# Zero fill on ScalarE, and twelve first results added before the last stage of a graph and mixture-of-experts kernel

## The chip, the cores and the metric

The kernel runs on one core of a Trainium2 chip. The metric is the device time of one execution in microseconds (us). It was timed three times; a separate execution was profiled. One core has TensorE (PE, matmul), VectorE (DVE), ScalarE (ACT), GpSimd (POOL) and SyncE (SP), which each run their own instruction stream and meet at semaphores, and 16 DMA engines.

## The reference

```python
x = x + gnn(layernorm(x), weight, bias, edge_index, edge_type)      # 3125 nodes x 256, 53125 edges, 8 relations
x = x + ffn(layernorm(x)[None], gate_w, gate_b, w1, w2, w3)[0]

def gnn(node_repr, weight, bias, edge_index, edge_types):
    h_all = jnp.einsum('ni,roi->rno', node_repr, weight)
    msgs = h_all[edge_types, src]
    return jax.ops.segment_sum(msgs, dst, num_segments=3125) + bias

def ffn(x, gate_w, gate_b, w1, w2, w3):                             # 16 experts, hidden 512
    probs = softmax(x @ gate_w + gate_b); top_probs, top_idx = top_k(probs, 2)
    top_probs = top_probs / sum(top_probs)
    hidden = silu(x @ w1[e]) * (x @ w2[e])
    return sum over the two experts e of a node of top_probs[e] * (hidden @ w3[e])
```

Every node thus gets its row after the graph layer, plus two weighted rows that its two experts computed.

## The kernel before

The 3125 nodes are handled as 25 node tiles (`TILES`) of 125 rows (`TP`). The work has four stages.

- **Start, about 0 to 72 us of the profile.** SP loads x into `acc` (five batches of five tiles) and the edge lists. VectorE turns a first list of edge sources (`early_src`) into floats (L959), TensorE turns them to partitions (L1544), VectorE writes them as indices `early_idx` (L965), and that releases GpSimd's first 37 indirect gathers of rows of x (L617: 25 into `held`, in the tile `part`, and 12 into `odd_held`). VectorE and ScalarE normalize the rows, in a high and a low half of 16 bits each, into `got`; SP stores them as a table `x_tab` and then loads the relation weights (L471). Part of this is the moments of the first ten gathered tiles (`held_moments(0)`, L1031), which VectorE computes before the edge keys and the last two batches of x. GpSimd also sets constants, and it clears `ffn` (L601, the zeros that are later stored over the table `y_tab`) and `logit` (L602).
- **Graph layer, to about 560 us.** One turn for each node tile: GpSimd gathers up to 17 chunks of 125 neighbour rows (L611), TensorE multiplies them with one-hot matrices (L1593), VectorE adds the windows into `store`, TensorE applies the relation weights (L1605).
- **Experts, to about 890 us.** Nodes are sorted by expert into slot tiles of 128 rows, in this input 58 of them (`final_j` is the last). `expert_tile` stands in the code of TensorE, ScalarE and VectorE, one call for each slot tile. In VectorE's, `low_hid` (L1442) works on the tile before, then `hid` is formed (L1454), `low_xs` (L1432) prepares the next tile, and `copy_y` (L1438) takes the result of the tile before out of PSUM bank 4. In ScalarE's, `high_hid` (L874), `store_y` (the DMA of a result tile to `y_tab`, L890), the Silu (L885), and `high_xs` (L868). TensorE's up product is L1759, its down product L1741, its turning of `hid` L1767. The experts use PSUM banks 0 to 4.
- **Sum, to the end.** `y_tab` holds a row for each (node, expert) pair. GpSimd gathers each node tile's lower row into `y1` (L694) and its higher row into `y2` (L707). For each node tile t ScalarE copies `acc` to PSUM (`keep_sum`, L920), VectorE adds the first result there (`add_first`, L1510) and then the second one into `acc` (`add_second`, L1519). SP stores 112 rows of the tile (L583) and ScalarE 13 rows (L929). `SUM_BANK` names the six PSUM banks for this, with one tile in each, so that add_first is ahead of add_second by four tiles. No bank beyond the experts' own is used for it before the last result was copied out: ScalarE issues the last `store_y` before the first `keep_sum`.

All engines work through their streams in the order in which the code is written; a wait holds everything that stands behind it on that engine.

## Time and profile before

| | before |
|---|---|
| median of 3 runs | 914.04 us (911.89 to 915.19) |
| the profiled execution's own time | 916.64 us |
| its span, first to last instruction | 914.8 us |
| busy: PE / POOL / DVE / ACT | 731.6 / 655.4 / 518.1 / 302.4 us |
| mean granted TensorE clock | 0.944 |

The span is 1.84 us shorter than the time of its own execution, and that execution was 2.60 us above the median of the three timed runs. Busy times are sums over stages in which different engines set the pace, so they do not say by themselves what one stage is worth.

### The profile page before, as it was taken

What the parts mean: (1) busy time and instruction counts of PE and PEld (TensorE: products, weight loads), DVE (VectorE), ACT (ScalarE), POOL (GpSimd) and SP (SyncE); (2) the same over time, 40 slices, a digit from 0 to 9 for tenths busy, and PEclk for the clock granted to TensorE, in tenths of its full rate; (3) what the DMA queues carried; (4) which work ended last, traced back from release to release, by engine and by line L of the source; (5) the groups of instructions that cost most, each with busy time, mean ns of one, the idle gap of its engine ahead of it and who ended that gap; (6) DMA issues with size and microseconds to landing.
All of it is one profiled execution on the core that took longest, in us unless ns stands there. A gap on an engine that the chain in (4) does not pass through costs nothing.

```text
span 914.8 us, 19945 instructions
## 1 busy us (share of the span) xinstructions
PE 731.6 (80%) x4626; PEld 623.0 (68%) x4627; DVE 518.1 (57%) x1444; ACT 302.4 (33%) x469; POOL 655.4 (72%) x609
## 2 busy tenths in 40 slices
PE   0136697888788898888879888689999999999980
PEld 0125586777677676777758676467888888788870
DVE  6887566545556446555446767874444444344438
ACT  5524234332333323343233523122333333233323
POOL 7777777777777777777777740359787886987772
PEclk9998799999999999999979998999999999999995
DMA  9875656433333333333364324176656655663546
GB/s 203 250 229 179 189 184 199 142 106 105 106 107 108 107 105 105 106 108 105 108 187 132 104 65 167 30 266 200 212 189 218 229 184 187 200 215 93 163 133 187
DMA packets 92526, 142.09 MB, mean 155 GB/s; under 512 B 13752, under 2 KB 67069, under 8 KB 92476
## 3 DMA queue, kind: packets, MB, share of 16 engines
q0 software_dynamic: 25440, 69.50, 26.1%
q1 hardware_dynamic: 50114, 56.92, 19.6%
q10 hardware_dynamic: 16922, 15.15, 5.2%
q14 instruction: 38, 0.31, 0.1%
q8 instruction: 12, 0.20, 0.1%
HBM read 108.59 MB, written 32.93 MB: 155 GB/s over the span
## 4 chain that ended last, share of the span: by engine, by line
PE 45%; POOL 22%; issue 14%; DMA 10%; DVE 7%; ACT 1%; DVEq 0%; POOLq 0%; SPq 0%; ACTq 0%
POOL got L611 20%; PE ps L1759 16%; PE ps L1741 9%; PE ps L1593 8%; PE ps L1605 6%; DMA got<-x_tab,gidx 6%; PE ps L1767 3%; DMA store<-in_L_gnn_weight 2%; PE ps L1725 1%; PE ps L1694 1%; DVE ps L1510 1%; POOL part L617 1%; DMA y_tab<-ffn 1%; DMA part<-in_x,early_idx 1%; POOL part L645 1%
## 5 line engine op out<-in xcount | busy, mean ns | idle before, releaser
L611 POOL DMA_INDIRECT got<-x_tab,gidx x383 | 366.4, 957 | 118.3 <-issue 108.9
L1593 PE MATMUL ps<-hot,got 125*128 125x256 f16 x1680 | 219.3, 290 | 79.7 <-DMA got<-x_tab,gidx 75.7
L1593 PEld LDWEIGHTS ps<-hot,got 125*128 125x128 f16 x1680 | 170.1, 104 | 122.9 <-issue 38.4
L1156 DVE TENSOR_TENSOR store<-store,ps 128x512 f32 x150 | 102.6, 684 | 179.2 <-PE ps L1593 146.2
L1759 PE MATMUL ps<-part,operands 128*128 x696 | 179.3, 407 | 4.9 <-DVE operands L1432 3.1
L1605 PE MATMUL ps<-part,store 128*128 128x256 f32 x800 | 181.9, 386 | 0.5 <-DVE acc L1167 0.5
L1605 PEld LDWEIGHTS ps<-part,store 128*128 128x128 f32 x800 | 152.5, 193 | 20.7 <-issue 0.6
L1759 PEld LDWEIGHTS ps<-part,operands 128*128 128x128 f32 x696 | 128.3, 191 | 32.5 <-issue 5.7
L1138 DVE TENSOR_SCALAR hot<-key_row,pass,drel 125x256 f16<-125x256 f16 x425 | 126.1, 362 | 7.5 <-ACT store L778 4.9
L1741 PE MATMUL ps<-part,operands 128*128 x696 | 97.9, 289 | 3.8 <-DVE operands L1442 3.6
L645 POOL TENSOR_TENSOR part<-store,part 128x2048 fp32r<-128x2048 f32 (+1 forms) x28 | 98.0, 3500 | 2.3
L787 ACT ACTIVATE dev<-mv,eps 125x1 f32<-125x1 f32 x25 | 7.4, 295 | 257.8 <-DVE mv L1174 257.8
L1741 PEld LDWEIGHTS ps<-part,operands 128*128 128x128 f32 x696 | 87.0, 189 | 4.5 <-issue 4.5
L1454 DVE TENSOR_TENSOR ffn<-ffn,ps 128x512 f32<-128x512 f32 x58 | 39.9, 687 | 83.1 <-PE ps L1759 79.4
L656 POOL DMA_INDIRECT x_sb<-x_tab,oct_idx x56 | 54.8, 979 | 21.8 <-issue 16.7
L804 ACT COPY store<-store 128x2480 f32<-128x2480 f32 x24 | 54.2, 2259 | 31.8 <-DVE store L1156 31.8
L874 ACT CAST operands<-ps 128x512 fp32r<-128x512 f32 x58 | 34.0, 587 | 91.7 <-PE ps L1767 91.7
L1442 DVE TENSOR_TENSOR operands<-ps,operands 128x512 fp32r<-128x512 f32 x58 | 40.0, 690 | 26.8 <-ACT operands L874 26.7
L885 ACT ACTIVATE ffn<-ps 128x512 f32<-128x512 f32 x58 | 34.7, 598 | 59.0 <-PE ps L1759 49.8
L1438 DVE COPY ffn<-ps 128x256 f32<-128x256 f32 x58 | 24.6, 425 | 51.1 <-PE ps L1741 31.1
L643 POOL TENSOR_SCALAR part<-store 128x2048 fp32r<-128x2048 f32 (+1 forms) x28 | 41.6, 1485 | 15.4 <-PE ps L1759 14.4
L782 ACT COPY store<-zero 128x2000 f32<-128x2000 f32 x25 | 46.9, 1875 | 0.0
(254 smaller groups left out, 685.8 us busy)
## 6 DMA issues: line engine op xcount, KB each, us to landing
store<-in_L_ffn_w SPq DMA_DIRECT2D x48, 512.0 KB, 4.8
part<-x_tab SPq DMA_DIRECT2D x625, 1.0 KB
y_tab<-ffn SPq DMA_DIRECT2D x9, 896.0 KB, 6.3
y_tab<-ffn ACTq DMA_DIRECT2D x58, 128.0 KB
xs_tab<-x_sb SPq DMA_DIRECT2D x14, 512.0 KB, 3.3
ffn<-xs_tab ACTq DMA_DIRECT2D x55, 128.0 KB
got<-x_tab,gidx POOLq DMA_INDIRECT x383, 2.8
acc<-in_x SPq DMA_DIRECT2D x5, 560.0 KB
```

The costliest lines, as they stand in the source:

```text
L611: nc.gpsimd.indirect_dma_start(got[:, c, :], None, x_tab, bass.IndirectOffsetOnAxis(ap=gidx[:, col:col + 1], axis=0)).then_inc(gathered[g] ...
L643: nc.gpsimd.tensor_scalar(high, whole, 1.0, 0.0, ALU.mult, ALU.add).then_inc(split_high, 1)
L645: nc.gpsimd.tensor_tensor(part[:, 2 * k + 1, at:at + cols], whole, high.bitcast(F32), ALU.subtract).then_inc(done, 1)
L656: nc.gpsimd.indirect_dma_start(xg[:, u, :], None, x2_tab, bass.IndirectOffsetOnAxis(ap=oct_idx[:, u:u + 1], axis=0)).then_inc(oct_got[u // ...
L782: nc.scalar.copy(buffer(i, SPAN - TP, SPAN), zero[:, 0:1].unsqueeze(1).to_broadcast([P, KT * RELS, TP])).then_inc(tail_clear, 1)
L804: nc.scalar.copy(buffer(i + 1, 0, SPAN - TP), buffer(i, TP, SPAN)).then_inc(moved_on, 1)
L1138: made = v.tensor_scalar(hot[0:CE, g % HOT, c - GROUPS[g][0], :], key_row[0:CE, :], pass0[0:CE, 0:1], drel[0:CE, bass.ds(turn * TC + c, 1) ...
L1156: v.tensor_tensor(window, window, ps[:, WIN_BANK[g], :].rearrange("p (q n) -> p q n", n=WIN), ALU.add).then_inc(win_added, 1)
L1593: last = mm(ps[:, WIN_BANK[g], k * KEYS:(k + 1) * KEYS], rows, hot[0:CE, g % HOT, c - c0, :], start=(c == c0 and a == 0), stop=(c == c1 - ...
L1605: last = mm(ps[:, bank, 0:DIM], sums[:, at, k, r, 0:P], wT[:, k, r * DIM:(r + 1) * DIM], start=(r == 0 and k == 0), stop=(r == RELS - 1 an ...
L1741: last = mm(ps[:, Y_BANK, 0:DIM], hidT[:, a, k, :], part3[:, bass.ds(at + b, 1), k, :].rearrange("p a n -> p (a n)"), start=(k == 0 and a ...
L1759: last = mm(ps[:, UP_BANK + w, :], xsT[:, a, k, :], part12[:, bass.ds(at + b, 1), w, k, :].rearrange("p a n -> p (a n)"), start=(k == 0 an ...
```

## The change

First, GpSimd's two memsets of `ffn` and `logit` are removed and ScalarE writes the same zeros, by copying a broadcast zero. Second, the sums are held two to a PSUM bank (`SUMS` = 12 places, `sum_at`), and ScalarE copies `acc` to PSUM two tiles at a time (`keep_sums`). Twelve tiles get their `add_first` earlier: three after `low_hid` in each of the last two expert tiles, five after the last `low_hid`, and one after the last `copy_y`. In what is left add_first is ahead by eight tiles. VectorE's and ScalarE's last pair of expert tiles stand behind their loops for it. The diff:

```diff
@@ -417,6 +417,8 @@
         WIN_BANK, MSG_BANK, T_BANK, GATE_BANK = (0, 1, 2, 5, 6, 7), 3, 4, 4
         UP_BANK, XS_BANK, HID_BANK, Y_BANK = 0, 2, 3, 4
         SUM_BANK = (5, 6, 7, 0, 1, 2)
+        SUMS = 2 * len(SUM_BANK)
+        SOON_SUMS = 3
 
         CHOICE_STEPS = 6
         SWEEP_STEPS = 2 * CHOICE_STEPS + 7
@@ -430,6 +432,10 @@
         def buffer(i, n0, n1):
 
             return sums[:, bass.ds(i % 2, 1), :, :, n0:n1].rearrange("p a k r n -> p (a k r) n")
+
+        def sum_at(t):
+            n = t % SUMS
+            return ps[0:TP, SUM_BANK[n // 2], n % 2 * DIM:(n % 2 + 1) * DIM]
 
         def low_hot(k, t):
 
@@ -598,8 +604,6 @@
             nc.gpsimd.iota(tile_i[:, :, :], pattern=[[1, TILES], [0, NG]], base=0, channel_multiplier=0).then_inc(iota_ready, 1)
             nc.gpsimd.iota(token_i[:, 0:2 * TILES], pattern=[[0, 2], [1, TILES]], base=-(TILES // 2), channel_multiplier=0).then_inc(iota_ready, 1)
             nc.gpsimd.iota(token_i[:, 2 * TILES:], pattern=[[0, 1]], base=0, channel_multiplier=1).then_inc(iota_ready, 1)
-            nc.gpsimd.memset(ffn[:, :], 0.0).then_inc(zeros_set, 1)
-            nc.gpsimd.memset(logit[:, :, :], 0.0).then_inc(acc_init, 1)
 
             def gather_turn(n, turn):
                 for g, (c0, c1) in enumerate(GROUPS):
@@ -718,6 +722,8 @@
             for n in range(2):
                 act.sem_inc(xs_in[n], (n + 1) * 16)
             act.wait_ge(zero_set, 1)
+            nc.scalar.copy(ffn[:, :], zero[:, 0:1].to_broadcast([P, ZT * DIM])).then_inc(zeros_set, 1)
+            nc.scalar.copy(logit[:, :, :].rearrange("p t e -> p (t e)"), zero[0:TP, 0:1].to_broadcast([TP, TILES * EXPERTS])).then_inc(acc_init, 1)
 
             def spread_x(n):
 
@@ -885,6 +891,14 @@
                 nc.scalar.activation(gate, ps[:, UP_BANK, :], ACT.Silu).then_inc(gate_ready, 1)
                 act.wait_ge(up2_done, j + 1)
                 high_xs(j + 1, 1 - u, load=load and not first)
+            def keep_sums(q):
+
+                t0, t1 = 2 * q, min(2 * q + 2, TILES)
+                if t0 >= SUMS:
+                    act.wait_ge(out_ready, t0 - SUMS + 2)
+                bank = ps[0:TP, SUM_BANK[q % len(SUM_BANK)], 0:(t1 - t0) * DIM].rearrange("p (t d) -> p t d", d=DIM)
+                nc.scalar.copy(bank, acc[:, t0:t1, :]).then_inc(first_sum, 1)
+
             def store_y(j):
                 act.wait_ge(y_ready, j + 2)
                 act.dma_start(y_tab[bass.ds(j * P, P), :], y_sb).then_inc(y_stored, 16)
@@ -901,31 +915,30 @@
             with act.Fori(1, early + (LAST_PAIRS - 1)) as i:
                 for u in range(2):
                     expert_tile(i, u)
-            for u in range(2):
-                expert_tile(early + (LAST_PAIRS - 1), u, load=False)
+            keep_sums(0)
+            keep_sums(1)
+            expert_tile(early + (LAST_PAIRS - 1), 0, load=False)
+            keep_sums(2)
+            expert_tile(early + (LAST_PAIRS - 1), 1, load=False)
             act.wait_ge(y_done, final_j + 1)
             high_hid(final_j)
             store_y(final_j - 1)
+            act.wait_ge(hid_ready, final_j + 1)
+            act.sem_inc(tiles_begun, 1)
+            act.wait_ge(xsT_ready, final_j + 2)
+            act.sem_inc(tiles_begun, 1)
+            for q in range(3, 6):
+                keep_sums(q)
             store_y(final_j)
             act.wait_ge(xs_in[0], pairs * 16)
             act.wait_ge(xs_in[1], pairs * 16)
             act.sem_inc(tiles_begun, 1)
 
-            banks = len(SUM_BANK)
-
-            def keep_sum(t):
-
-                if t >= banks:
-                    act.wait_ge(out_ready, t - banks + 1)
-                nc.scalar.copy(ps[0:TP, SUM_BANK[t % banks], 0:DIM], acc[:, t, :]).then_inc(first_sum, 1)
-
             p0, p1 = SPREAD[1]
-            for t in range(banks):
-                keep_sum(t)
             for t in range(TILES):
                 act.wait_ge(out_ready, t + 1)
-                if t + banks < TILES:
-                    keep_sum(t + banks)
+                if t % 2 and t - 1 + SUMS < TILES:
+                    keep_sums((t - 1 + SUMS) // 2)
                 act.dma_start(out[t * TP + p0:t * TP + p1, :], acc[p0:p1, t, :]).then_inc(out_stored, 16)
             act.wait_ge(y_stored, (pairs * 2 + 1) * 16)
             act.sem_inc(tiles_begun, 1)
@@ -1442,10 +1455,12 @@
                 v.tensor_tensor(hidT[:, 1, :, :], ps[:, HID_BANK, :].rearrange("p (k n) -> p k n", k=HT),
                                 hidT[:, 0, :, :].bitcast(F32), ALU.subtract).then_inc(hidT_ready, 1)
 
-            def expert_tile(i, u, first=False, tables=None):
+            def expert_tile(i, u, first=False, firsts=(), tables=None):
                 j = i * 2 + u
                 if not first:
                     low_hid(j - 1)
+                    for t in firsts:
+                        add_first(t)
                     if tables:
                         tables()
                 dve.wait_ge(gate_ready, j + 1)
@@ -1459,7 +1474,7 @@
                     copy_y(j - 1)
 
             final_j = dve.value_load(final[0:1, 0:1], min_val=0, max_val=SLOT_TILES - 1)
-            pairs = dve.value_load(pairs_i[0:1, 0:1], min_val=EXPERTS // 2, max_val=SLOT_TILES // 2)
+            early = dve.value_load(early_i[0:1, 0:1], min_val=EXPERTS // 2 - LAST_PAIRS, max_val=SLOT_TILES // 2 - LAST_PAIRS)
             low_xs(0)
             order_tables()
             positions()
@@ -1505,27 +1520,30 @@
 
             def add_first(t):
                 dve.wait_ge(y_got[t], 16)
-                dve.wait_ge(first_sum, t + 1)
-                at = ps[0:TP, SUM_BANK[t % len(SUM_BANK)], 0:DIM]
-                v.scalar_tensor_tensor(out=at, in0=y1[0:TP, t, :], scalar=wts2[:, 0, t:t + 1],
-                                       in1=at, op0=ALU.mult, op1=ALU.add).then_inc(part_done, 1)
-
-            with dve.Fori(3, pairs) as i:
+                dve.wait_ge(first_sum, t // 2 + 1)
+                v.scalar_tensor_tensor(out=sum_at(t), in0=y1[0:TP, t, :], scalar=wts2[:, 0, t:t + 1],
+                                       in1=sum_at(t), op0=ALU.mult, op1=ALU.add).then_inc(part_done, 1)
+
+            with dve.Fori(3, early + (LAST_PAIRS - 1)) as i:
                 for u in range(2):
                     expert_tile(i, u)
+            for u in range(2):
+                expert_tile(early + (LAST_PAIRS - 1), u, firsts=range(u * SOON_SUMS, (u + 1) * SOON_SUMS))
+
             def add_second(t):
                 dve.wait_ge(part_done, t + 1)
                 dve.wait_ge(y_got[t], 2 * 16)
                 v.scalar_tensor_tensor(out=acc[:, t, :], in0=y2[0:TP, t % YR, :], scalar=wts2[:, 1, t:t + 1],
-                                       in1=ps[0:TP, SUM_BANK[t % len(SUM_BANK)], 0:DIM], op0=ALU.mult, op1=ALU.add).then_inc(out_ready, 1)
+                                       in1=sum_at(t), op0=ALU.mult, op1=ALU.add).then_inc(out_ready, 1)
 
             low_hid(final_j)
+            for t in range(2 * SOON_SUMS, SUMS - 1):
+                add_first(t)
             copy_y(final_j)
-            ahead = len(SUM_BANK) - 2
-            for t in range(ahead):
-                add_first(t)
+            add_first(SUMS - 1)
+            ahead = SUMS - 4
             for t in range(TILES):
-                if t + ahead < TILES:
+                if SUMS <= t + ahead < TILES:
                     add_first(t + ahead)
                 add_second(t)
 
```

The order of instructions shows three places; line numbers behind the change are up to 18 higher. First GpSimd's stream at its start, where the gathers of `early_idx` come; before:

```order
L597 IOTA hot 128x256
L598 IOTA tile_i 1x150
L599 IOTA token_i 128x50
L600 IOTA token_i 128x1
L601 MEMSET ffn 128x1792
L602 MEMSET logit 125x400
L617 DMA part<-in_x,early_idx 128x256 x25
```

And GpSimd's stream in the changed kernel:

```order
L603 IOTA hot 128x256
L604 IOTA tile_i 1x150
L605 IOTA token_i 128x50
L606 IOTA token_i 128x1
L621 DMA part<-in_x,early_idx 128x256 x25
L621 DMA odd_held<-in_x,early_idx 128x256 x12
```

The two memsets are gone. ScalarE's stream begins, in the changed kernel, with them and a table load of their own, where it began with the load and the square root:

```order
L725 ACT_TABLE_LOAD
L725 COPY ffn<-zero 128x1792 [waits zero_set]
L726 COPY logit<-zero 125x400
L732 ACT_TABLE_LOAD
L732 ACTIVATE dev<-mv,eps 125x5 [waits stats_done]
```

Two copies and one table load were added ahead of the first real work. Second, VectorE's stream around the last `low_hid` (L1442) and the last `copy_y` (L1438); before:

```order
L1442 TENSOR_TENSOR operands<-ps,operands 128x512
L1436 REGISTER_ALU
L1437 REGISTER_ALU
L1438 COPY ffn<-ps 128x256
L1510 SCALAR_TENSOR_TENSOR ps<-x_sb,wts,ps 125x256 x5
L1519 SCALAR_TENSOR_TENSOR acc<-store,wts,ps 125x256
L1510 SCALAR_TENSOR_TENSOR ps<-x_sb,wts,ps 125x256
```

And in the changed kernel, from the last tile's `low_hid` (L1455) on:

```order
L1455 TENSOR_TENSOR operands<-ps,operands 128x512
L1524 SCALAR_TENSOR_TENSOR ps<-x_sb,wts,ps 125x256 x5
L1449 REGISTER_ALU
L1450 REGISTER_ALU
L1451 COPY ffn<-ps 128x256
L1524 SCALAR_TENSOR_TENSOR ps<-x_sb,wts,ps 125x256
L1536 SCALAR_TENSOR_TENSOR acc<-store,wts,ps 125x256 x4
L1524 SCALAR_TENSOR_TENSOR ps<-x_sb,wts,ps 125x256
L1536 SCALAR_TENSOR_TENSOR acc<-store,wts,ps 125x256
```

Five first adds moved ahead of the last copy, and one stands behind it; two groups of three stand further up, between `low_hid` and `hid` of the last two tiles. Third, ScalarE's stream of the changed kernel from the end of its loop of expert tiles, with what each instruction waits for:

```order
L915 COMPARE_AND_BRANCH
L900 COPY ps<-acc 125x512 x2
L885 ISA
L880 CAST operands<-ps 128x512 [waits hid_turned,y_done]
L904 ISA [waits y_ready]
L904 DMA y_tab<-ffn 128x256
L889 REGISTER_ALU
L891 ACTIVATE ffn<-ps 128x512 [waits hid_ready,up1_done]
L873 REGISTER_ALU [waits up2_done]
L874 CAST operands<-ps 128x256 [waits xs_turned]
L900 COPY ps<-acc 125x512
L880 CAST operands<-ps 128x512 [waits hid_turned,y_done]
```

Two double copies now stand ahead of `high_hid` of the last tile but one, and one ahead of that of the last tile; three more come before the last `store_y`.

## Rows read from the trace of the kernel before

**Rows 1.** The page, part 4: the chain that ended last, by engine.

```profile
PE 45%; POOL 22%; issue 14%; DMA 10%; DVE 7%; ACT 1%; DVEq 0%; POOLq 0%; SPq 0%; ACTq 0%
```

**Rows 2.** Timeline, 2 to 8 us: start, duration, instruction, [idle before, its releaser].

```profile
2.74 2.20 DVE L959 CAST store<-store 37x125 f32<-37x125 int32 x1 [0.70 <-DMA store<-in_src]
...
2.92 1.58 POOL L601 MEMSET ffn<- 128x1792 f32 x1
...
4.45 0.42 POOL L602 MEMSET logit<- 125x400 f32 x1
...
6.01 1.16 POOL L617 DMA_INDIRECT part<-in_x,early_idx  x1 [1.14 <-DVE early_idx L965]
```

**Rows 3.** Timeline of DVE, 0 to 75 us.

```profile
25.69 3.37 DVE L1031 BATCH_NORM_STATS2 stat<-part 125x6 f32<-125x256 f32 x10 [3.55 <-DMA part<-in_x,early_idx]
...
29.64 0.45 DVE L1018 CAST store<-store 85x625 f32<-85x625 int32 x1
```

**Rows 4.** DMA issues in 6.0 to 6.2 and 17.6 to 17.8 us; last number: us to landing.

```profile
part<-in_x,early_idx POOLq DMA_INDIRECT x1, 8.8
...
part<-in_x,early_idx POOLq DMA_INDIRECT x1, 8.0
```

**Rows 5.** The chain that ended last, 0 to 110 us: start, duration, what.

```profile
46.00 16.96 DMA store<-in_L_gnn_weight
```

**Rows 6.** Waits of POOL over the whole span: us in total, times, longest.

```profile
POOL got L611 <- issue: 108.9, 357, 0.3
...
POOL got L611 <- PE ps L1593: 9.4, 26, 1.8
```

**Rows 7.** Timeline of ACT, 0 to 75 us.

```profile
9.22 1.28 ACT L726 ACT_TABLE_LOAD   x1 [9.22 <-DVE mv L983]
...
71.60 3.92 ACT L778 COPY store<-zero 128x4480 f32<-128x4480 f32 x1 [1.65 <-issue]
```

**Rows 8.** Timeline of DVE, 855 us to the end.

```profile
879.79 0.69 DVE L1454 TENSOR_TENSOR ffn<-ffn,ps 128x512 f32<-128x512 f32 x1 [1.49 <-PE ps L1759]
...
890.26 0.42 DVE L1438 COPY ffn<-ps 128x256 f32<-128x256 f32 x1 [2.18 <-PE ps L1741]
891.91 2.05 DVE L1510 SCALAR_TENSOR_TENSOR ps<-x_sb,wts,ps 125x256 f32<-125x256 f32 x5 [1.22 <-ACT ps L920]
893.87 0.47 DVE L1519 SCALAR_TENSOR_TENSOR acc<-store,wts,ps 125x256 f32<-125x256 f32 x1
...
909.71 2.04 DVE L1519 SCALAR_TENSOR_TENSOR acc<-store,wts,ps 125x256 f32<-125x256 f32 x5
```

**Rows 9.** Timeline of ACT, 855 us to the end (ACTq: its DMA issues).

```profile
875.39 0.35 ACTq L864 DMA_DIRECT2D ffn<-xs_tab  x1
876.99 0.59 ACT L874 CAST operands<-ps 128x512 fp32r<-128x512 f32 x1 [1.50 <-PE ps L1767]
...
886.98 4.22 ACTq L890 DMA_DIRECT2D y_tab<-ffn  x2
891.41 1.90 ACT L920 COPY ps<-acc 125x256 f32<-125x256 f32 x6 [4.05 <-DVE ffn L1438]
...
894.45 0.60 ACTq L929 DMA_DIRECT2D out<-acc  x1
```

**Rows 10.** Timeline of PE, 855 us to the end.

```profile
888.40 1.73 PE L1741 MATMUL ps<-part,operands 128*128 x12 [1.72 <-DVE operands L1442]
```

**Rows 11.** Instructions on `y_tab`, 830 to 915 us: duration, first and last start; landing.

```profile
L694 POOL DMA_INDIRECT x_sb<-y_tab,pos x25: 942/946/999, 835.6 to 865.7; - x25
L707 POOL DMA_INDIRECT store<-y_tab,pos x25: 942/946/949, 866.9 to 898.5; - x25
...
DMA to landing us min/median/max: 2.7/2.9/4.1
```

**Rows 12.** SP's out stores, 910.2 us to the end; windows, with DMA share and GB/s last.

```profile
910.21 2.49 SPq L583 DMA_DIRECT2D out<-acc  x5
...
900.00:902.00 2.00, 0.00 (x0) 0.00 (x0) 2.00 (x6) 1.04 (x3) 0.00 (x0) 0.50 0.92 283
```

## The prediction

> **What bounds the kernel now.** I read the page's chain first, then the timeline of every engine at the two places that the change touches. The chain [rows 1] shows TensorE and GpSimd as the two long parts: GpSimd's gathers through the graph layer, TensorE through the experts. VectorE has 7%, most of it after the last expert tile. The change touches neither long part; it touches what comes before and behind them. So the two questions are whether an earlier start is handed on through some 840 us, and what bounds the last 25 us.
>
> *Start.* GpSimd's train of gathers begins at 6.01 us and waited 1.14 us for VectorE's `early_idx` [rows 2]. The reader should look at what held VectorE: its cast L959 covers only 37x125 numbers, yet takes 2.20 us and ends at 4.94. A cast of 85x625, five times as many in each row, takes 0.45 us [rows 3]. Beside the slow one stand GpSimd's two memsets, from 2.92 to 4.87 us [rows 2]; the cast ends 0.07 us after the second. I read it as one engine being held by the other until the memsets end. The Trainium skill, "SBUF — State Buffer", section "Who interferes with whom", says that certain VectorE copies and casts and any GpSimd instruction take one shared port pair exclusively, and whoever comes second is fully blocked; the trace agrees in that 2.20 against 0.45 us.
>
> From there the chain runs on. VectorE is idle 3.55 us until the tenth gather has landed, at 25.69 [rows 3]. That gather was issued at 17.65 and took 8.0 us, the first one 8.8 [rows 4]; so the time to land hardly depends on when a gather is issued, though the queues are full then. Behind it come edge keys, the last batches of x, and at 46.00 the relation weights, 16.96 us on the path [rows 5]. In the graph layer GpSimd's gathers wait 357 times 0.3 us for nothing the profile shows, and for TensorE only 9.4 us in all [rows 6]: the train is nearly back to back, TensorE follows it, and nothing there is tied to a fixed time.
>
> *End.* After the last `copy_y` at 890.26 VectorE has 50 adds to do and no idle gap worth the name: first ones at 891.91, last ones from 909.71 for 2.04 us, so to 911.75 [rows 8]. One add takes 0.47 us but starts (2.04 - 0.47) / 4 = 0.39 us after the one before. Stores follow; the span ends at 914.8, 3.05 us after the last add. The last y2 gather starts at 898.5, and the longest landing is 4.1 us [rows 11]: it is there by about 902.6, nine us before it is used. VectorE is the bound.
>
> **The change part by part.**
>
> *Memsets off GpSimd.* They end at 4.87 while GpSimd cannot gather before 6.01, so their own time is hidden; the worth is in the cast. With GpSimd's iotas over by 2.92 to 3.0 us, the cast (issued at 2.74) should end at about 3.05 in place of 4.94. The rest, transpose, copy, semaphores, took 6.01 - 4.94 = 1.07 us and stays. First gather at about 4.1: 1.9 us earlier. From below: nothing, if the cast is slow for a reason of its own, or if the queues, full of loads of x, land the tenth gather no sooner. From above: the idle time that waits for the gather, 3.55 us. I take 1.9, since the latencies of 8.8 and 8.0 us [rows 4] are near enough to constant, and 1.9 is less than 3.55. After that it is carried on, since each later step on the chain is released by the one before.
>
> *Zeros on ScalarE.* 4480 columns took 3.92 us there [rows 7]; 1792 and 400 columns at that rate are 1.57 and 0.35 us, with the new table load of 1.28 us some 3.3 us in all, from about 2 us on (or the load even earlier). ScalarE's first work is at 9.22 us, having waited 9.22 us [rows 7]. Cost nothing; the cover is about 3.9 us.
>
> *Copies in the last two tiles (ScalarE).* A copy of 256 columns takes about (1.90 - 0.38) / 5 = 0.30 us more than the one before [rows 9], a double one, with 256 more columns at 3.92 / 4480 us each, about 0.53. Two of them begin when the DMA issue of 875.39 is over, at 875.74, and end near 876.9. `high_hid` starts at 876.99, after 1.50 us of idle time [rows 9]. If the exit from the loop adds some tenths, `high_hid` is late by that; behind it queue a store and the Silu, and VectorE's `low_hid` waits for it. TensorE would feel it only when its slack is gone, and it is busy with the up products then. Cost 0, bound 0.5 us.
>
> *Three adds in each of the two tiles (VectorE).* 3 x 0.39 = 1.2 us in an idle gap of 1.49 us ahead of `hid` [rows 8]. Hidden, by 0.3 us. The `hid` instruction (0.69 us) would be late next if the gap does not hold, and TensorE's turning behind it. Bound 0.5 us for each tile.
>
> *Five adds after the last `low_hid`.* TensorE's last down product starts at 888.40 and takes 1.73 us [rows 10]; VectorE is idle 2.18 us before `copy_y` [rows 8]. The adds need 5 x 0.39 = 1.95 us from about 888.2, once ScalarE's three double copies (from 887.4, after the store issued at 886.98) give them their places: to 890.2. `copy_y` is not late, or by 0.1 us. The last `store_y` now stands behind three copies that end at about 889.1; it is issued at 890.9 anyway.
>
> *The rest.* Before, VectorE went from `copy_y` (890.26) to the first add at 891.91, since ScalarE had to store and to copy first, 1.22 us of it idle [rows 8]. Now the twelfth add comes at about 890.60. Gain 1.31 us. Adds left: 50 - 11 = 39, so 11 x 0.39 = 4.3 us less. A new wait: after four second adds the thirteenth first add needs a double copy that ScalarE may start only when two second adds are done (891.9) and its first store of a row is issued (0.60 us [rows 9]): ready near 892.9, wanted at 892.56. Cost 0.35 us. Later copies have four adds of lead. Last add ends at 911.75 - 1.31 - 4.3 + 0.35 = 906.5 or a little less; y2 is there since 902.6.
>
> *Stores.* With eight tiles ahead, the last nine second adds come 0.39 us apart, where before it was five. SP issued its last five stores from 910.21 to 912.70, one in 2.49 / 5 = 0.50 us [rows 12]: slower than 0.39. Before it fell back by 4 x 0.11 = 0.4 us; now 8 x 0.11 = 0.9. Cost 0.5 us. The most that the queues moved at this stage is 283 GB/s at a share of 0.92 [rows 12]; nine tiles of 125 KB in 9 x 0.39 us would be 328. Queues that can't follow cost 9 x 128 / 283 = 4.1 us for 3.5, another 0.6 us; it overlaps the first, and I take 0.5 for both, bound 1.5.
>
> **The sum.** Start -1.9; first add earlier -1.3; eleven adds -4.3; new wait +0.35; stores +0.5: -6.7 us, with the small bounds above at nothing. The profiled execution goes from 916.64 to about 909.9 (span 914.8 to 908.1). The median of the runs shown stood 2.60 us below that execution, so 914.04 becomes 907.4. Of the three runs, two differ by 3.3 us; less than 0.3% (2.7 us) cannot be told from no change here.
>
> **The rivals.**
>
> *The start gives nothing back* (0.15). For it: while x is loaded the queues are full, and a gather needs 8 us; if it lands when the loads issued ahead have drained, an earlier issue is only a longer wait. Against: the first gather and the tenth have nearly the same latency. Only the end is left: 914.04 - 4.8 = 909.2 us. The same time results if the cast stays slow.
>
> *The end becomes a matter of stores* (0.13). SP's 0.50 us and the queues' 283 GB/s, with y2 gathers still beside them, set the pace instead of the adds: bound 1.5 us in place of 0.5, perhaps another 0.5 from the four early second adds. 908.4 to 908.9 us.
>
> *The insertions reach TensorE* (0.07). `high_hid` and `hid` late in both tiles, 0.5 us each time, `copy_y` late too: +1 to +1.5 us, so 908.4 to 909 us.
>
> *The adds do no good where they stand* (0.02): if add 6 to 11 wait for ScalarE until `copy_y`, that is late and their time comes back: +2 us and more, with a lost start about 911.5, within 0.3%.
>
> *Slower* (0.02). VectorE's stream now waits for y1 of tiles 0 to 5 inside the last expert tiles; `hid`, `low_xs` and TensorE stand behind that wait. Were the sixth y1 gather to land after about 879.4 us, each us of it would go on the path; slower by 0.3% needs a landing 6.7 + 2.7 us later, at about 888.8. The gathers start at 835.6 and 25 take until 865.7 [rows 11], so the sixth starts near 841.9 and with 4.1 us has landed at 846. Cover 33 us: only a much later y table would bring it about. It would give 917 us and up.
>
> **How the numbers follow.** My forecast, both gains whole, has 0.61: 907.4, alone from 906.2 (less lost at the stores, a start gain of 2.2) to 908.6. The range is to hold 8 in 10 and takes in the lost start and the store case: 905.3 to 910.2, which leaves out the adds case and the slower one, and runs beyond the mean of three runs by about 1 us on the low side. Faster by over 0.3% (below 911.3): the first four cases, 0.95; within 0.3%: 0.03; slower: 0.02.
>
> **What the changed profile would show.** Right: the cast of 37x125 under 0.5 us, the first gather near 4.1, VectorE's moments (L1031 before) near 23.8, the weights issued near 44.1, the whole graph layer and the experts some 1.9 us earlier; in the last two tiles no idle time of TensorE before its turning of `hid`; then 0.35 us idle at the thirteenth first add, and a last add some 5.2 us earlier relative to the last `copy_y` of before. Wrong: a cast that still takes 2 us; a tenth gather that lands at 25.7 with 10 us latency; TensorE gaps near 880; SP's stores still being issued 2 us after the last add. A run of the granted clock that falls elsewhere in the graph layer could shift the total by a us or two with none of these steps wrong.

## The result, and the profile after

The changed kernel takes 910.42 us (median of 12 runs), the kernel before 915.18 us (12 runs, 911.9 to 920.4). One of the twelve runs of the changed kernel took 1263 us (without it the median is 909.84, and the range 905.0 to 913.6), and in two of the four groups of experiments below every kernel, the one before too, took some 1200 us for a reason that no run tried, so times are compared inside a group only. The ratio is 0.9947, with a 95% interval of 0.9928 to 0.9966: 4.85 us faster, and anything from 3.1 to 6.6. The forecast was 907.4 with a range from 905.3 to 910.2, a gain of 6.7 us. The direction was right. The median of the twelve lies 0.2 us above the range, that of the eleven 0.4 us inside it, so the time alone hardly says whether the sum was wrong. A part of the distance is the base: the three runs shown before had a median of 914.04, the twelve of the comparison 915.18.

The profiled execution of the changed kernel took 911.70 us with a span of 909.3, against 916.64 and 914.8. So there are 5.5 us to be found in the two traces. I read the start first. These rows are from the engines' timelines after the change, 0 to 80 us (SPq: SyncE's DMA issues), in order of time.

```profile
1.30 1.28 ACT L725 ACT_TABLE_LOAD   x1 [1.30 <-PEq L1830]
2.75 0.22 DVE L972 CAST store<-store 37x125 f32<-37x125 int32 x1 [0.70 <-DMA store<-in_src]
4.03 1.16 POOL L621 DMA_INDIRECT part<-in_x,early_idx  x1 [1.03 <-DVE early_idx L978]
5.89 19.27 SPq L466 DMA_DIRECT2D acc<-in_x  x4
24.62 3.37 DVE L1044 BATCH_NORM_STATS2 stat<-part 125x6 f32<-125x256 f32 x10 [3.84 <-DMA part<-in_x,early_idx]
37.29 1.09 ACT L745 ACTIVATE got<-acc,shift_n,rstd 125x256 f16<-125x256 f32 x2 [1.20 <-DMA x_tab<-got]
44.38 1.65 ACT L753 COPY store<-ps 1x425 f32<-1x425 f32 x2
45.93 0.84 SPq L477 DMA_DIRECT2D store<-in_L_gnn_weight  x1
62.09 6.12 PE L1575 MATMUL ps<-ident,store 128*128 128x128 f32 x32 [10.21 <-DMA store<-in_L_gnn_weight]
66.70 2.23 ACT L761 COPY part<-ps 128x512 f32<-128x512 f32 x4
71.26 9.00 PE L1611 MATMUL ps<-hot,got 125*128 125x256 f16 x54 [3.05 <-DVE hot L1151]
74.81 0.94 POOL L615 DMA_INDIRECT got<-x_tab,gidx  x1 [3.12 <-PE ps L1611]
```

The cast takes 0.22 us where it took 2.20 [rows 2]. It still starts at 2.75, beside GpSimd's last iotas, and no memset is there to hold it. The first gather starts at 4.03 in place of 6.01. Both are as forecast. The Trainium skill, "SBUF — State Buffer", section "Who interferes with whom", says that a VectorE copy or cast that uses both port pairs and a GpSimd instruction shut each other out of the shared pair, and that the one that issues first gets it. The traces agree with the first half, by 2.20 against 0.22 us. They don't show the second: before the change the cast starts at 2.74 and the first memset at 2.92, and yet the cast is the one that is held.

Then the lead of 2 us wears off, in two places. The first is the landing of the gathers. The tenth is issued at 15.50, 2.15 us earlier than before, but it takes 9.1 us to land in place of 8.0 [rows 4]. In every profile near 910 us that has the early gathers and where the tenth one's landing can be read it took 8.5 to 9.1 us, in e2, which hasn't them, 7.7:

```profile
part<-in_x,early_idx POOLq DMA_INDIRECT x1, 9.1
```

So the moments behind it are at 24.62, only 1.07 us earlier than [rows 3] has them. The second place is SyncE's stores of `x_tab`. SyncE is done with issuing its last four loads of x at 25.16 in place of 24.34. In the eight profiles near 910 us that have the early gathers this is at 24.6 to 25.4 us, in the two without them at 23.8 and 24.3; I put it down to the gathers' packets on the same DMA engines, which were busy without a gap from 6 to 24 us already before the change (DMA share 1.02 to 1.12). So the stores of `x_tab` are later, and ScalarE has a wait that it didn't have before, 1.20 us, until 37.29. At its copy of the edge lines, which releases VectorE's planning of the graph layer, it stands at 44.38; before that was

```profile
44.47 1.64 ACT L747 COPY store<-ps 1x425 f32<-1x425 f32 x2
```

The lead at that place is 0.09 us, and SyncE issues the relation weights at 45.93, before at 46.00 [rows 5]: 0.07 us. The train of GpSimd's gathers, which doesn't wait for that copy, goes on 2 us early until about 70 us, then stands 3.12 us before the first gather of the second turn, because TensorE's first window (71.26, before 72.27) has not freed a buffer. Before the change it stood there too:

```profile
75.82 0.95 POOL L611 DMA_INDIRECT got<-x_tab,gidx  x1 [1.83 <-PE ps L1593]
```

The first window starts 2.3 us after the last of ScalarE's eight copies of the turned weights, in this profile (68.93 to 71.26) and in all ten near 910 us. In both profiles here those copies wait for the weights, which TensorE could use 16.2 us after their issue, and before the change 17.0 us after it. So the 1.0 us by which the window leads comes mostly from a load that happened to be faster and not from the gathers. From there GpSimd leads by 1.0 us, by 1.1 at the end of the graph layer, and by 0.5 when the last `hid` of the experts is made (884.19, before 884.68).

The end, from VectorE's timeline:

```profile
882.62 1.26 DVE L1524 SCALAR_TENSOR_TENSOR ps<-x_sb,wts,ps 125x256 f32<-125x256 f32 x3
884.19 0.69 DVE L1469 TENSOR_TENSOR ffn<-ffn,ps 128x512 f32<-128x512 f32 x1 [0.31 <-issue]
...
887.79 2.06 DVE L1524 SCALAR_TENSOR_TENSOR ps<-x_sb,wts,ps 125x256 f32<-125x256 f32 x5 [0.20 <-ACT ps L900]
889.76 0.42 DVE L1451 COPY ffn<-ps 128x256 f32<-128x256 f32 x1
890.10 0.48 DVE L1524 SCALAR_TENSOR_TENSOR ps<-x_sb,wts,ps 125x256 f32<-125x256 f32 x1
890.49 1.65 DVE L1536 SCALAR_TENSOR_TENSOR acc<-store,wts,ps 125x256 f32<-125x256 f32 x4
892.42 0.49 DVE L1524 SCALAR_TENSOR_TENSOR ps<-x_sb,wts,ps 125x256 f32<-125x256 f32 x1 [0.28 <-ACT ps L900]
```

The three adds lie in the gap before `hid`, with 0.31 us left of the 1.49 of [rows 8]. Five more lie before the last `copy_y`, which comes 5.57 us after the last `hid`, as before (890.26 - 884.68 = 5.58). The thirteenth add waits 0.28 us. The last add ends at 905.83, 16.07 us after `copy_y` started; before it was 911.75 - 890.26 = 21.49. The span ends 3.45 us behind the last add, where it was 3.03. From the last `hid` to the end of the span it is 25.1 us, and was 30.1: the end gives 5.0 us. With 0.5 of lead left at that `hid`, this is the 5.5 between the traces.

### The profile page after: what moved, and what is told of

The parts are those of the page before. It is cut to its first block, busy times and chain, and to the rows that moved or that the text cites. A ratio compares the mean times of both kernels' runs of the same rounds, so it can differ in the third digit from the quotient of the medians.

```text
span 909.3 us, 19921 instructions
## 1 busy us (share of the span) xinstructions
PE 733.3 (81%) x4626; PEld 622.9 (69%) x4627; DVE 517.1 (57%) x1444; ACT 303.4 (33%) x460; POOL 652.9 (72%) x607
## 4 chain that ended last, share of the span: by engine, by line
PE 47%; POOL 17%; issue 13%; DMA 9%; DVE 8%; SPq 3%; ACT 1%; DVEq 1%; POOLq 0%; ACTq 0%
POOL got L615 16%; PE ps L1777 16%; PE ps L1611 9%; PE ps L1759 8%; PE ps L1623 8%; DMA got<-x_tab,gidx 6%; PE ps L1785 3%; SPq L466 2%; DMA y_tab<-ffn 2%; PE ps L1743 1%; PE ps L1712 1%; DMA x_tab<-got 1%; DVE acc L1536 1%; DVE hot L1151 1%; ACT got L745 1%
## 5 line engine op out<-in xcount | busy, mean ns | idle before, releaser
L891 ACT ACTIVATE ffn<-ps 128x512 f32<-128x512 f32 x58 | 34.7, 598 | 62.8 <-PE ps L1777 46.2
L1455 DVE TENSOR_TENSOR operands<-ps,operands 128x512 fp32r<-128x512 f32 x58 | 40.1, 691 | 26.8 <-ACT operands L880 26.7
L1451 DVE COPY ffn<-ps 128x256 f32<-128x256 f32 x58 | 24.6, 425 | 52.0 <-PE ps L1759 29.2
```

## The experiments

There were sixteen runs of eight kernels, in four groups (e1 to e4, e5 to e8, e9 to e12, e13 to e16); those of one group share a chip and the runs of the kernel before. Each profile gives two marks to compare by: ScalarE's line copy near 44 us (how early the graph layer can be planned) and the stretch from the last `hid` to the end of the span (what the end costs).

**e1: the kernel before with the zero fill alone.**

```diff
-            nc.gpsimd.memset(ffn[:, :], 0.0).then_inc(zeros_set, 1)
-            nc.gpsimd.memset(logit[:, :, :], 0.0).then_inc(acc_init, 1)
...
+            nc.scalar.copy(ffn[:, :], zero[:, 0:1].to_broadcast([P, ZT * DIM])).then_inc(zeros_set, 1)
+            nc.scalar.copy(logit[:, :, :].rearrange("p t e -> p (t e)"), zero[0:TP, 0:1].to_broadcast([TP, TILES * EXPERTS])).then_inc(acc_init, 1)
```

> The kernel before with only the zero fill moved to ScalarE. Theory A: the first gather goes at 4.03 us as in the changed kernel, but the lead of 2 us shrinks to about 1 us at the first window of the graph layer (71.3 in place of 72.3), because SP's loads of x take 0.8 us longer and the table stores behind them land late; total 0.5 to 1.1 us under the kernel before. Rival 1: the lead is carried on whole, total 1.9 us under. Rival 2: nothing is left, total within 0.3 us.

912.03 us against 913.29: ratio 0.9986 (0.9966 to 1.0007), so 1.3 us faster, between 3.1 faster and 0.6 slower. The cast takes 0.22 us, the first gather is at 4.02, the moments at 24.65, and again there is the new wait and no lead at the line copy:

```profile
37.58 1.09 ACT L739 ACTIVATE got<-acc,shift_n,rstd 125x256 f16<-125x256 f32 x2 [0.99 <-DMA x_tab<-got]
44.66 1.65 ACT L747 COPY store<-ps 1x425 f32<-1x425 f32 x2
```

The interval holds the theory (0.5 to 1.1 us), the lead carried on whole (1.9 us) and nothing at all, so the time doesn't decide between them.

**e2: the changed kernel with the memsets back on GpSimd** (the reverse of e1's edit).

> The changed kernel with the two memsets back on GpSimd. Theory A: the end's gain is whole by itself: from the last copy_y to the last add 16.1 us in place of 21.5, and 3.4 us from there to the end in place of 3.05; total 5.0 us under the kernel before. The cast of 37x125 takes 2.2 us again. Rival: the end's gain needs the start's, or is partly lost at the stores: 3.5 us or less under.

910.5 us, ratio 0.9962 (0.9942 to 0.9983): 3.5 us faster than before (1.6 to 5.3). Last `hid` to end 25.1 us, as in the changed kernel: the end's gain doesn't need the start's. The cast takes its 2.21 us again, so with e1 it is shown that the memsets beside it make it slow:

```profile
2.74 2.21 DVE L972 CAST store<-store 37x125 f32<-37x125 int32 x1 [0.69 <-DMA store<-in_src]
```

ScalarE does not wait for `x_tab<-got`, as in the kernel before, and its line copy is at 44.05, earlier than in the changed kernel. Its relation weights happen to land by 59.95, and the first window starts at 69.91; the kernel before has the same instructions up to there and needs until 72.27. So single profiles differ by 2 us at the first window, and the lead of 1.0 us seen there is no proof.

**e3: the changed kernel with three small loads later**, after the third store of `x_tab` in place of ahead of the first.

```diff
-            sp.dma_start(bias[:, :], ...).then_inc(small_in, 16)
-            sp.dma_start(gw_sb[:, :, :], ...).then_inc(small_in, 16)
-            sp.dma_start(gb_sb[:, :], ...).then_inc(small_in, 16)
...
+                if n == 2:
+                    sp.dma_start(bias[:, :], ...).then_inc(small_in, 16)
+                    sp.dma_start(gw_sb[:, :, :], ...).then_inc(small_in, 16)
+                    sp.dma_start(gb_sb[:, :], ...).then_inc(small_in, 16)
```

> The changed kernel with SP's three small loads (bias, gate weights, gate bias) issued after the third store of x_tab instead of ahead of the first. Theory A: they stood for 2.3 us ahead of the stores (25.20 to 27.48 us), so the first store lands 1 to 2 us earlier, ScalarE's wait of 1.20 us at 37.29 is gone, the lead at 44.4 us becomes about 1.1 in place of 0.1, and the first window starts near 70.3; total about 1 us under the changed kernel. Rival: the queues are full, the store lands at the same time for its bytes, and nothing changes (within 0.3 us).

907.08 us (7 runs), ratio 0.9935 (0.9907 to 0.9964). The wait of ScalarE is gone and the line copy is at 43.47. So about 1 us of the lead does die at the stores of `x_tab`, and can be had back there. Whether it is worth anything in the whole is e15's question.

**e4: no adds inside the last two tiles** (`SOON_SUMS = 0`: the six adds go behind the last `low_hid`).

> The changed kernel with no first adds inside the last two expert tiles: eleven of them after the last low_hid instead of five. Theory A: eleven need 4.3 us where 2.1 are free, so the last copy_y starts 2.3 us late and the total is 2.3 us over the changed kernel, that is 2.7 us under the kernel before; this says that the six adds inside the tiles are hidden and worth their 0.39 us each. Rival: the end is bound by stores, so that the late adds cost less than 1 us.

909.57 us, ratio 0.9961 (0.9940 to 0.9982). The eleven adds in one piece make `copy_y` late:

```profile
887.06 4.40 DVE L1524 SCALAR_TENSOR_TENSOR ps<-x_sb,wts,ps 125x256 f32<-125x256 f32 x11
891.37 0.42 DVE L1451 COPY ffn<-ps 128x256 f32<-128x256 f32 x1
```

It starts 7.62 us after the last `hid` in place of 5.57, and the end takes 27.3 us in place of 25.1. So the place inside the tiles is worth 2.1 us by the profiles. The last tiles stand 4.89 us apart at `hid` with the adds inside and without them, so they cost nothing there. The times are too near to show it: 910.5 for e2, whose end has the adds inside but whose start is the old one, and 909.57 here.

**e5 to e12: four kernels, twice.** In these two groups the kernel before took 1204.1 and 1203.4 us, and the first window of the graph layer stood at 98 to 104 us, so nothing of the start is read from them. The kernels were: the relation weights' load moved up (e5, e9; see e13), two buffers for y (e6, e10; see e14), the out stores of tiles 17 to 22 in three pairs (e7, e11), these three all with e3's edit too, and the change as it is (e8, e12).

```diff
-            for t in range(TILES):
-                sp.wait_ge(out_ready, t + 1)
-                sp.dma_start(out[t * TP + p0:t * TP + p1, :], acc[p0:p1, t, :]).then_inc(out_stored, 16)
+            for t, n in OUT_PARTS:
+                sp.wait_ge(out_ready, t + n)
+                sp.dma_start(out[t * TP:(t + n) * TP, :].rearrange("(t p) d -> p t d", p=TP)[p0:p1, :, :],
+                             acc[p0:p1, t:t + n, :]).then_inc(out_stored, 16)
```

The edit shown is that of e7 and e11 on SyncE; ScalarE's stores have the same one. What was expected, in the order e5 to e12:

> The changed kernel with the small loads after the third store of x_tab (as in e3) and, right behind them, the load of the relation weights (w_raw), which stood at the end of SyncE's list. Theory 'the start's lead dies at the weights': in four profiles the weights' first transposes stand at 60 to 63 us while the work ahead of them is done at 44 us, so the first window at 70 to 72 us is set by when the weights land. With the load some 3 us after the x loads they should be there by 50 us, TensorE's transposes should stand at 50 us or earlier, the first window should stand at 68.5 to 70 us (then VectorE's chain holds it), and the kernel should be 1 to 2 us below e3 with less spread. Rival 'the full queues only change places': the 1.3 MB or so in front of the last two x_tab stores makes these and the gathers of got that wait for them later by as much, the first window stays at 70.5 to 72, and the time is that of e3 within 1 us or above it.

> The changed kernel with the small loads later (as in e3) and two buffers for the results y of a slot tile (the second is xn2, free by then), each with its own semaphore, so that VectorE's copy of tile j waits for the store of tile j-2 in place of j-1. Theory 'the run-to-run loss in the expert phase is VectorE behind late y stores': the copies' waits on DMA y_tab<-ffn vanish from the trace, the stretch from hid of tile 4 to hid of tile 37 falls from 162.3 us (e3) to 33 x 4.89 = 161.4 us, the one at tiles 0 to 4 from 25.4 us by some 2 us, and the kernel is 2 to 4 us below e3 (903 to 905). Rival 'PE sets the pace': the waits vanish and TensorE's tiles stand at the same distance as before, within 1 us of e3. Second rival: SyncE's and GpSimd's weight loads of the next expert, which the stores wait behind, are what is late, and the stall moves to the gate or to the splits of the weights: no gain either, but a new wait is named at hid.

> The changed kernel with the small loads later (as in e3) and the out stores of tiles 17 to 22 issued as three pairs instead of six, on each of the two queues; it moves the same bytes. From the last add to the end of the span e3 takes 3.54 us. If the predicted +0.5 us at the end is issue-bound (each issue on SyncE takes about 0.5 us, and the last ones stand in line behind each other), the stretch falls to about 3.0 and the kernel by 0.5 us. If it is the transfer itself and its landing, the stretch stays at 3.4 to 3.6 and the time is that of e3.

> The changed kernel once more, on the same chip as e5 to e7, as the bar for them. Theory: 0.5% below the kernel before, 909.5 to 911.5 us if this chip is like the first one; first window at 70 to 72 us with a wait of ScalarE on x_tab<-got at 37 us of 0.9 to 1.3 us; last add to end 3.5 us, last copy of y to last add 16.1 us.

> The kernel of e5 once more. On the chip of e5 to e8 every kernel took some 1200 us: SyncE's loads of far rows took 20 to 27 us a turn there in place of 10 to 11, and the graph layer waited for them, so nothing at the start could be read. On a chip where the kernel before takes some 914 us the expectations of e5 stand: theory, weights' transposes at 50 us or earlier, first window at 68.5 to 70 us, 1 to 2 us below the kernel of e3; rival, first window at 70.5 to 72 us and no gain, or a loss, because the load stands in front of the last x_tab stores.

> The kernel of e6 once more, for the same reason. Theory: no wait of the copy of y for DMA y_tab<-ffn, the stretch from hid of tile 4 to hid of tile 37 at 161.4 us or less, hid 0 to hid 4 shorter by about 2 us, 2 to 4 us below e3's kernel. First rival: TensorE sets the pace and the time stays within 1 us. Second rival: a new wait takes the place, named at hid or at the splits of the weights.

> The kernel of e7 once more, for the same reason. There the stretch from last add to end was 3.72 us with pairs and 3.54 with single stores, 1 run each, so now I take it that pairs bring nothing: 3.4 to 3.8 us and the time of e3's kernel within its interval. If issues bound the end it would be 3.0.

> The kernel of e8 once more, as the bar for e9 to e11 on their chip: 0.3 to 0.7% below the kernel before; copy of y to last add 16.1 us, last add to end 3.5 us, ScalarE's wait for x_tab<-got at 37 us of 0.9 to 1.3 us, first window at 70 to 72 us.

The stretch from the last `hid` to `copy_y` is not steady there (5.56 to 7.76 us), but what stands behind `copy_y` is as it was. Last add to end of span: 3.72 and 3.50 us with pairs, 3.57 and 3.48 with single stores (e8, e12). With pairs SyncE's last issue starts 0.13 us after the last add, with single stores 0.96 and 0.87 us after it, and the end doesn't come earlier, so the 3.5 us are not set by SyncE's issues. The ratios tell little: e5 1.0019 (0.9986 to 1.0053) and e9 1.0002 (0.9965 to 1.0040), e6 0.9981 (0.9956 to 1.0006) and e10 0.9994 (0.9959 to 1.0029), e7 0.9973 (0.9944 to 1.0003), e11 0.9993 (0.9957 to 1.0029), e8 0.9986 (0.9954 to 1.0018), e12 0.9954 (0.9911 to 0.9997). Copy of y to last add is 16.06 or 16.07 us in all eight. e5, e6, e9 and e10 were run again at some 910 us, as e13 and e14; e7 and e11 were not.

**e13: the relation weights' load early**, right behind e3's small loads.

```diff
                 if n == 2:
...
+                    sp.dma_start(w_raw, w_rel.rearrange("r (a p) i -> p (r a) i", p=P)).then_inc(w_in, 16)
-            sp.dma_start(w_raw, w_rel.rearrange("r (a p) i -> p (r a) i", p=P)).then_inc(w_in, 16)
```

> The kernel of e5. Theory: weights' transposes at 50 us or earlier, first window at 68.5 to 70 us, 1 to 2 us below e15. Rival: the load stands in front of the last x_tab stores, the first window is at 70.5 us or later, and the time is e15's or above. In the runs at 1200 us the rival's sign was there: first window at 103 us against 98 us without the edit.

912.66 us, ratio 0.9991 (0.9975 to 1.0007), in a group where the kernel before took 914.19: 5.4 us slower than e15, the same kernel without this edit. The rival won, and more clearly than I had put it. TensorE's and GpSimd's timelines:

```profile
52.51 5.90 PE L1576 MATMUL ps<-ident,store 128*128 128x128 f32 x28 [1.78 <-DMA store<-in_L_gnn_weight]
65.27 1.11 PE L1576 MATMUL ps<-ident,store 128*128 128x128 f32 x4 [6.87 <-ACT part L762]
69.33 6.84 PE L1612 MATMUL ps<-hot,got 125*128 125x256 f16 x36 [2.95 <-DVE hot L1152]
...
58.23 0.95 POOL L616 DMA_INDIRECT got<-x_tab,gidx  x1 [5.91 <-issue]
```

The weights are there at 52.5 in place of 60.4, and the first window moves by 0.45 us only (e15: 69.78): their last transposes now wait for VectorE's moments, by way of ScalarE. But the first gather of `got`, which needs all of `x_tab`, starts at 58.23, where e15 has

```profile
52.64 1.18 POOL L616 DMA_INDIRECT got<-x_tab,gidx  x1 [0.30 <-issue]
```

The profile puts the 5.91 us down to "issue"; that it is the last stores of `x_tab` behind the 2 MB of weights is what the edit shows, since nothing else was moved. These 5.6 us stay: the first gather of the second turn is 5.3 us later than in e15 (78.63 against 73.34), the last one of the layer 5.5 us (538.97 against 533.48). In this kernel GpSimd goes through the second turn without a wait for TensorE, so what bounds the graph layer here is when the first gather of `got` starts. In the changed kernel it is not: there GpSimd waits 3.12 us at that place, and the second turn starts 3.55 us behind the first window. The two traces agree in that the later of the two sets the layer's pace from there.

**e14: two buffers for y**, each with a semaphore, on top of e3.

```diff
-        y_sb = ffn[:, 2 * HIDDEN:2 * HIDDEN + DIM]
+        y_sb = (ffn[:, 2 * HIDDEN:2 * HIDDEN + DIM], xn2[:, :])
...
-            def copy_y(j):
+            def copy_y(j, u, i):
                 dve.wait_ge(y_done, j + 2)
-                dve.wait_ge(y_stored, (j + 1) * 16)
-                v.tensor_copy(y_sb, ps[:, Y_BANK, 0:DIM]).then_inc(y_ready, 1)
+                dve.wait_ge(y_stored[u], (i + 1) * 16)
+                v.tensor_copy(y_sb[u], ps[:, Y_BANK, 0:DIM]).then_inc(y_ready, 1)
```

> The kernel of e6. Theory: no wait of the copy of y for DMA y_tab<-ffn, hid of tile 4 to hid of tile 37 at 161.4 us, hid 0 to hid 4 down by about 2 us, 2 to 4 us below e15. Rival: TensorE sets the pace (its tiles stand 4.89 us apart), the waits go and the time stays within 1 us of e15.

906.68 us (6 runs), ratio 0.9916 (0.9894 to 0.9937): the same as e15 and e16. The groups by line, VectorE, 590 to 908 us, busy and mean ns, then idle time and its releasers; e16 (the change as it is) first, e14 second:

```profile
L1469 DVE TENSOR_TENSOR ffn<-ffn,ps 128x512 f32<-128x512 f32 x58 | 39.8, 687 | 76.0 <-PE ps L1777 72.8 <-ACT ffn L891 2.6 <-issue 0.6
L1451 DVE COPY ffn<-ps 128x256 f32<-128x256 f32 x58 | 24.6, 424 | 52.0 <-PE ps L1759 27.5 <-DMA y_tab<-ffn 24.6
```

```profile
L1474 DVE TENSOR_TENSOR ffn<-ffn,ps 128x512 f32<-128x512 f32 x58 | 39.8, 687 | 82.3 <-PE ps L1782 81.7 <-issue 0.6
L1456 DVE COPY ffn<-ps 128x256 f32<-128x256 f32 x29 | 12.3, 424 | 18.1 <-PE ps L1764 18.1
L1456 DVE COPY xn<-ps 128x256 f32<-128x256 f32 x29 | 12.3, 424 | 19.2 <-PE ps L1764 19.2
```

24.6 us of waits for stores of y are gone, and came back in part as waits for TensorE. From `hid` of tile 4 to that of tile 37 it is 162.2 us in e14, 162.7 in e16 and 162.3 in e3. So the waits for stores cost nothing that can be seen, and TensorE's pace is what is left; I had taken the late stores for 2 to 4 us, and that was wrong.

**e15 and e16: e3's kernel and the change as it is, in the group of e13 and e14.**

> The kernel of e3: ScalarE's wait for x_tab<-got at 37 us gone, its line copy at 43.5 us, 0 to 3 us below e16 (e3 stood 0.12% under the change's own first ratio, with intervals of 0.3 to 0.4%).

> The changed kernel as it is: 0.3 to 0.7% below the kernel before, last copy of y to last add 16.1 us, last add to end 3.5 us, ScalarE's wait for x_tab<-got at 37 us of 0.9 to 1.3 us, first window at 70 to 72 us.

e15: 907.22 us (6 runs), ratio 0.9928 (0.9902 to 0.9954). e16: 906.89 us (6 runs), ratio 0.9921 (0.9902 to 0.9939). In ScalarE's timelines, e16 then e15, the small loads cost what they cost before:

```profile
37.18 1.09 ACT L745 ACTIVATE got<-acc,shift_n,rstd 125x256 f16<-125x256 f32 x2 [1.12 <-DMA x_tab<-got]
44.26 1.65 ACT L753 COPY store<-ps 1x425 f32<-1x425 f32 x2
```

```profile
35.91 1.09 ACT L746 ACTIVATE got<-acc,shift_n,rstd 125x256 f16<-125x256 f32 x2 [0.20 <-DMA x_tab<-got]
43.15 1.65 ACT L754 COPY store<-ps 1x425 f32<-1x425 f32 x2
```

1.1 us of lead at 43 us, and no difference between the medians that could be told from none. So no version that beats the changed kernel was found.

## Why the prediction was off, step by step

*What the cast waits for, and the first gather*: right (0.22 us, 4.03 us; 0.22 and 2.21 in e1 and e2). *Zeros on ScalarE at no cost*: right. Its two copies and the second table load end at 6.0 us, and its first work starts at 9.19, where it was 10.52 before, since that load no longer stands in front of it.

*The start's term, -1.9 us*: this is what failed, in both of its premises. "I take 1.9, since the latencies of 8.8 and 8.0 us are near enough to constant": the tenth gather was issued 2.15 us earlier and landed 1.07 us earlier, after 9.1 us in place of 8.0. "After that it is carried on, since each later step on the chain is released by the one before": the later steps are not all behind the gathers. Some are behind the loads and stores of x, which share the queues with the gathers. The weights were to be issued near 44.1; they were at 45.93, before at 46.00, and at 45.6 in e2, whose gathers are not early. In the profiles with early gathers (after, e1, e4, e16) the line copy is at 44.38, 44.66, 44.19 and 44.26, with ScalarE's new wait of 1.0 to 1.2 us in each; in the two without (before, e2) it is at 44.47 and 44.05, without that wait. Of 2.0 us nothing is left there. The bound "if the queues, full of loads of x, land the tenth gather no sooner" was in the text, and the rival on it had 0.15; what I had not seen is that x's own transfers would be late in exchange. What of the 2 us goes on is what the train of gathers keeps: the first gather of `got` starts at 51.97 (after), 51.76 (e16) and 52.69 (e1), before at 53.97. e13 shows that this mark does carry to the end when it moves by 5.6 us; but in the changed kernel the train stands at the second turn until TensorE's window gives it a buffer. The prediction had read GpSimd's waits for TensorE as small (9.4 us in all); the longest of them, 1.8 us [rows 6], stood at that very place, so the window had been the later of the two already. The 1.0 us that came through is the window's. By time, e1 has the start at 1.3 us, from 3.1 down to -0.6. A value of 1.9 isn't excluded, nor is nothing.

*First add earlier -1.3, eleven adds -4.3, new wait +0.35*: 5.25 us forecast from `copy_y` to the last add, 5.42 measured in the profile after, with the wait at 0.28. Right, and the same in every kernel with the edit (16.06 or 16.07 us).

*Stores +0.5*: 0.42 in the profile after, between 0.3 and 0.7 in the other seven with the edit near 910 us, and 0.2 in e1, which hasn't it. The size was about right. SyncE did fall back as forecast (its last issue starts 0.88 us after the last add, before 0.51), but that isn't what the end waits for: with pairs it starts 0.13 us after it, and the stretch is no shorter (e7, e11).

*Insertions at no cost*: right. `copy_y` is 5.57 us behind `hid` (before 5.58; 5.56 to 5.81 in the others that have them, near 910 us); e4 shows 2.1 us for the place outside.

*The sum.* By profile, the start gave 0.5 at the last `hid` and the end 5.0, where -1.9 and -4.8 were forecast. By time the whole change was measured twice near 910 us: -4.85 us (3.1 to 6.6) and, in e16, -7.2 us (5.6 to 9.0, as 914.19 times 0.0061 and 0.0098); e8 and e12 have it at -1.7 us (from 5.5 faster to 2.2 slower) and -5.5 us (0.4 to 10.7), too wide to help. The forecast of -6.7 is 0.1 us outside the first interval and inside the second. So it is the traces, not the medians, that say that the start's term was too large, and that the change's time agrees with the forecast in e16 doesn't speak for that term. The rival in which the start gives nothing back had 909.2 us: nearer than the forecast to the first comparison (910.4, or 909.8), and farther from e16.

*What stays open.* How much of a lead at the graph layer's start reaches the end. From the last gather of `got` to the last `hid` single profiles took between 343.3 (e13) and 347.9 us (after), with the same instructions, and a lead of 1 us is lost in that: e15's profiled execution ended 3.5 us ahead of e16's, while their medians are the same. I did not find which wait makes these differences; e14 speaks against late stores of y.

## What to carry to other kernels

An engine freed early at the start is worth only what the slowest of all its partners gives: when the queues are full, an earlier transfer makes another later, so follow each chain that uses the queue to the point where they meet, and price the lead there. A wait that is small in the sum can still be the one at the place where the lead must pass (1.8 us of 9.4 here): look where the longest of them stands. Work put into an idle gap in front of a step that the bound engine releases is as good as free as long as it is shorter than the gap; the same work behind the last such step costs its full time. And a large waiting time on an engine that is not the bound (24.6 us here) can be removed whole without any gain.

## What the runs showed of the hardware

A VectorE cast of 37x125 numbers took 2.20 and 2.21 us beside GpSimd's memsets (before, e2), and 0.22 to 0.25 us without them in the other eight profiles near 910 us.

The tenth indirect gather of 125 rows took 7.7 to 9.1 us from issue to landing while x was loaded, against 2.7 to 4.1 us for the DMA work on the table of y in the last stages [rows 11]. Issued 2.15 us earlier, it landed 1.07 us earlier. In that time SyncE needed 17.8 to 19.4 us to issue its last four loads of x.

The load of the relation weights, issued at 44.7 to 46.2 us in nine profiles near 910 us, was there 14.4 to 17.0 us later. Issued between the stores of `x_tab` it made the first gather that needs these stores 5.6 us later (e13 against e15), and the kernel 5.4 us slower.

Two executions of the same instructions can stand 2.4 us apart at the first window (69.91 in e2, 72.27 before), so a lead of 1 us in one pair of profiles shows nothing.
